# New step orders, three projections in a second PSUM bank, 26 warm-up matmuls, and the int8 result taken out of PSUM by ScalarE: an attention and int8 layer on one core

## What is computed

```python
q, k, v = x @ Wq + bq, x @ Wk + bk, x @ Wv + bv      # 16 query heads, 4 key/value heads, 16 wide
q, k = rope(q), rope(k)                              # per token
p = softmax(causal(q @ k.T * 0.25))                  # 4 query heads share one key/value head
x = layernorm(x + (p @ v) @ Wo)
scale = max(max(abs(x)), 1e-7) / 127.0               # per token
acc = clip(round(x / scale), -128, 127) @ weight.T   # int8 x int8
h = (acc * scale * w_scale + bias).astype(float16)   # w_scale and bias per output column
out = layernorm(x + h)
```

## Time and profile before

| | |
|---|---|
| median of 3 runs | 174.61 us (174.49 to 174.62) |
| the profiled execution's own time | 174.22 us |
| its span, first to last instruction | 172.3 us |
| around the span | 1.9 us |
| mean granted TensorE clock | 0.957 |
| busy in the span | PE 147.3, DVE 140.8, ACT 123.0, POOL 85.7 us |
| in the list: first reduction X0, first exponential E0, end of E159 | 12.59, 19.56, 156.25 us |

### The profile page before, as it was taken

How to read it: one execution, slowest core, us unless ns; L and a number is a source line. 1 busy time by engine, 2 the same in 40 slices (tenths; PEclk the granted TensorE clock), 3 DMA queues, 4 the chain that set the end, 5 groups by cost and what they waited for, 6 DMA issues and landing times. The chain is left out here.

```text
span 172.3 us, 4469 instructions
## 1 busy us (share of the span) xinstructions
PE 147.3 (85%) x1552; PEld 87.3 (51%) x1552; DVE 140.8 (82%) x345; ACT 123.0 (71%) x231; POOL 85.7 (50%) x191
## 2 busy tenths in 40 slices
PE   1768999999999999999999989999999988893330
PEld 0154464565665556656676456655666554551100
DVE  3408789898899599899899789989999997787582
ACT  3244577887797879898988776989878898993000
POOL 1051794224078868213899996032488504465111
PEclk9999999999999999999999999999999999997555
DMA  5986000000000001000000101000001200001101
GB/s 138 259 142 186 2 5 0 4 4 0 10 4 0 6 0 65 1 6 1 2 8 0 56 12 59 8 0 8 0 2 47 80 4 2 2 4 61 61 0 61
DMA packets 5463, 5.63 MB, mean 33 GB/s; under 512 B 1217, under 2 KB 4674, under 8 KB 5442
## 3 DMA queue, kind: packets, MB, share of 16 engines
q1 hardware_dynamic: 5298, 5.16, 10.9%
q10 hardware_dynamic: 144, 0.20, 0.4%
HBM read 3.12 MB, written 2.10 MB: 30 GB/s over the span
## 5 line engine op out<-in xcount | busy, mean ns | idle before, releaser
L415 ACT ACTIVATE prob<-score_ps 128x512 bf16<-128x512 f32 x160 | 89.6, 600 | 16.8 <-PE score_ps L616 8.2
L507 DVE TENSOR_REDUCE nmax<-front_ps 128x1 f32<-128x320 f32 (+21 forms) x137 | 87.6, 680 | 13.2 <-PE front_ps L660 12.3
L612 PE MATMUL score_ps<-qkA 128*128 128x512 bf16 x160 | 57.9, 379 | 0.9 <-ACT prob L415 0.5
L658 PE MATMUL front_ps<-qkA 128*128 128x384 bf16 (+9 forms) x176 | 50.6, 334 | 1.7 <-DVE nmax L507 1.4
L627 PEld LDWEIGHTS mix_ps<-qkv,prob 128*128 128x128 bf16 x640 | 26.1, 96 | 14.3 <-ACT prob L415 3.5
L660 PE MATMUL front_ps<-tab 128*128 128x32 bf16 (+2 forms) x176 | 32.3, 187 | 0.0
L627 PE MATMUL mix_ps<-qkv,prob 128*128 128x17 bf16 x640 | 30.2, 171 | 1.3 <-ACT prob L415 1.2
L658 PEld LDWEIGHTS front_ps<-qkA 128*128 128x128 bf16 x176 | 17.2, 98 | 16.6 <-issue 6.8
L616 PE MATMUL score_ps<-tab 128*128 128x512 bf16 x64 | 24.2, 378 | 0.0
L424 ACT ACTIVATE qkA<-side_ps 128x1024 bf16<-128x1024 bf16 x16 | 16.4, 1024 | 5.5 <-PE side_ps L649 5.3
L354 POOL TENSOR_TENSOR rot<-qkv,tab 128x320 bf16<-128x320 bf16 x14 | 10.4, 745 | 18.6 <-ACT qkv L420 18.6
(11 more groups left out here) (61 smaller groups left out, 175.6 us busy)
## 6 DMA issues: line engine op xcount, KB each, us to landing
out<-fo SPq DMA_DIRECT2D x7, 256.0 KB, 2.2
xt<-in_xT SPq DMA_DIRECT2D x1, 768.0 KB, 6.3
qkA<-peakT SPq DMA_DIRECT2D x32, 4.0 KB
xt<-in_xT SPq DMA_DIRECT2D x2, 128.0 KB, 3.0
bfc<-in_bias SPq DMA_DIRECT2D x2, 128.0 KB, 7.4
out<-fo SPq DMA_DIRECT2D x2, 128.0 KB, 1.7
tab<-in_table SPq DMA_DIRECT2D x1, 232.0 KB, 3.1
wqkv<-in_wqkv_in ACTq DMA_DIRECT2D x1, 192.0 KB
```

Source lines behind the costliest of these rows:

```text
L415: act.activation(prob[:, u % PROB_RING, :].rearrange("p (h t c) -> p t h c", h=GH, c=SUB), score_ps[u % SCORE_RING][:, :].rearrange("p (t ...
L507: dve.tensor_reduce(to, src, AX.X, ALU.max, negate=True).then_inc(max_ok, 1)
L612: mm = pe.matmul(score_ps[u % SCORE_RING][:, :].rearrange("p (t c) -> p t c", c=TOK), qkA[:, n, GH + g, TOK * j:TOK * (j + 1)], qkA[:, n, ...
L658: pe.matmul(bank, qkA[:, n, t, TOK * i:TOK * (i + 1)], qkA[:, n, GH + g:GH + g + fit, 0:wide], start=True, stop=False)
```

## The change

Nothing of the arithmetic's result is meant to change. These parts are edited:

1. Before it waits for the weights, PE issues 26 matmuls of the one-row tile `ones` with itself (128 columns) into `mix_ps`.
2. P1, P2 and P3 go into `dense_ps` instead of `side_ps`.
3. Steps l0 to l5 move from DVE to ACT. There the two tiles are multiplied with the token's scale alone (an fp32 copy of it, `qscf`, written by one more small DVE operation in B0 to B5). POOL's H0 to H5 begin with one more operation on 128x512 fp32, the product with the column's scale. l6, l7 and l8 stay as they were.
4. The five lists are reordered. `rden` has two slots.

The steps n and d of ACT, r of DVE and N of POOL, which the diff also defines, stand in no list, and `NORM_FAST` is 0, so that they do nothing here.

```diff
+LINEAR_ACT = True
+HEAD_TILES = (1, 2, 3, )
+WARM = 26
+NORM_FAST = 0
 ORDER = {
     "tensor": """
-        P0 P1 P2 T0 T1 F0 F1 F2 F3 F4 T2 F5 F6 G0 F7 F8 F9 P3 F10 F11 F12 P4 S0 S1 F13 F14 F15 P5 S2 F16 F17 T3 F18 S3 F19 F20
+        P0 P1 P2 T0 P3 T1 F0 F1 F2 F3 T2 F4 F5 F6 P4 F7 F8 F9 G0 F10 T3 F11 F12 P5 F13 F14 S0 F15 G1 S1 F16 F17 F18 S2 S3 T4
...
-        S135 U6 W132 W133 W134 S136 W135 S137 M6 G15 W136 S138 W137 S139 W138 S140 W139 S141 W140 S142 S143 D5 W141 S144 W142
-        W143 S145 L5 S146 S147 S148 D6 S149 W144 W145 S150 L6 S151 W146 W147 S152 W148 W149 W150 W151 S153 U7 W152 S154 W153
-        S155 W154 S156 M7 S157 W155 S158 W156 S159 W157 W158 W159 U8 M8 D7 L7 D8 L8
+        W131 S135 F175 S136 U6 W132 S137 W133 W134 W135 S138 W136 M6 G15 S139 S140 W137 W138 S141 W139 S142 W140 S143 W141
+        S144 W142 D5 S145 W143 S146 S147 L5 S148 S149 W144 W145 W146 W147 D6 S150 W148 S151 U7 W149 S152 W150 S153 W151 M7
+        S154 W152 S155 W153 S156 W154 S157 W155 S158 W156 S159 W157 L6 W158 W159 D7 U8 M8 L7 D8 L8
     """,
     "scalar": """
-        p0 p1 p2 t0 t1 t2 f0 p3 p4 E0 E1 p5 E2 t3 E3 f1 t4 E4 E5 p6 E6 E7 t5 E8 E9 f2 E10 E11 t6 E12 E13 E14 E15 p7 E16 E17
+        p0 p1 p2 t0 p3 t1 t2 p4 f0 t3 p5 E0 f1 E1 E2 E3 t4 E4 E5 p6 E6 E7 t5 E8 E9 p7 E10 E11 f2 t6 E12 E13 t7 E14 E15 u0 p8
...
-        E146 E147 E148 E149 E150 E151 E152 E153 E154 u7 E155 E156 E157 E158 E159 u8
+        E143 E144 E145 E146 E147 l5 E148 E149 E150 E151 u7 E152 E153 E154 E155 E156 E157 E158 E159 u8
     """,
     "vector": """
...
-        N13 X135 X136 B5 s6 q5 a6 B6 d5 q6 l5 N14 d6 l6 Z5 H6 s7 Z6 a7 B7 N15 Y6 q7 s8 a8 B8 d7 q8 l7 H7 d8 Z7 l8 H8 Y7 Z8 Y8
+        B5 s6 q5 a6 B6 d5 q6 N14 d6 s7 Z5 a7 B7 q7 l6 N15 d7 H6 s8 Z6 a8 B8 Y6 l7 q8 H7 d8 Z7 l8 H8 Y7 Z8 Y8
     """,
     "gpsimd": """
-        R2 w0 K0 R3 K1 R4 R5 K2 R6 R7 K3 K4 K5 m0 R8 Q0 R9 K6 R10 H0 z0 Y0 R11 K7 m1 K8 Q1 K9 m2 R12 Q2 R13 H1 H2 K10 z1 Y1 z2
-        R14 Y2 R15 m3 K11 K12 Q3 K13 m4 Q4 H3 K14 H4 z3 Y3 z4 Y4 m5 K15 Q5 m6 H5 z5 Y5 m7 z6 m8 z7 z8
+        R2 R3 K0 R4 w0 K1 R5 R6 K2 R7 R8 K3 m0 R9 K4 Q0 K5 R10 H0 K6 z0 Y0 R11 m1 K7 Q1 K8 R12 m2 K9 R13 Q2 H1 R14 K10 z1 H2
+        Y1 z2 m3 Y2 K11 R15 K12 Q3 m4 K13 Q4 H3 H4 K14 z3 Y3 z4 Y4 m5 K15 Q5 m6 H5 m7 z5 Y5 m8 z6 z7 z8
     """,
     "sync": """
-        g0 g1 g2 g3 g4 g5 g6 O0 g7 g8 g9 O1 g10 O2 g11 g12 g13 g14 O3 O4 g15 O5 O6 O7 O8
+        g0 g1 g2 g3 g4 g5 g6 O0 g7 g8 g9 g10 O1 O2 g11 g12 g13 g14 O3 O4 g15 O5 O6 O7 O8
     """,
 }
...
+def in_dense(step):
+    return step[0] in "UMDL" or step[0] == "P" and step[1] in HEAD_TILES
+SIDE_USES = [step for step in steps("tensor") if step[0] in "PTG" and not in_dense(step)]
+DENSE_USES = [step for step in steps("tensor") if in_dense(step)]
...
+        def project_bank(u):
+            if u in HEAD_TILES:
+                return dense_ps, dense_full, dense_free, dense_at("P", u)
+            return side_ps, side_full, side_free, side_at("P", u)
...
                 elif kind == "H":
...
+                    if LINEAR_ACT:
+                        pool.tensor_tensor(fo[:, part, :], fo[:, part, :], wsc[:, :].unsqueeze(1).broadcast_to([128, len(ms), HID]),
+                                           ALU.mult).then_inc(fw_ok, len(ms))
+                        pool.wait_ge(fw_ok, done)
...
+                elif kind == "l":
+                    ms, part, done = tiles_of(u)
+                    act.wait_ge(dense_full, dense_at("L", u) + 1)
+                    for m in ms:
+                        one = act.activation(fo[:, m, :], dense_ps[:, (m - ms[0]) * HID:(m - ms[0] + 1) * HID], ACT.Copy,
+                                             scale=qscf[:, m:m + 1])
+                        one.then_inc(dense_free if m == ms[-1] else fo_ok, 1)
...
                     dve.wait_ge(qsc_ok, done)
+                    if LINEAR_ACT and u not in FAST:
+                        dve.tensor_copy(qscf[:, part], qsc[:, part])
...
         @block.tensor
         def _(pe):
             pe.wait_ge(ones_set, 1)
+            for _ in range(WARM):
+                pe.matmul(mix_ps[:, 0:128], ones[:, :], ones[:, :], start=True, stop=True)
             pe.wait_ge(weights_in, 16 * 2)
```

More of the change, by code:

```diff
@@ L86 @@
[L86 to L97, removed]
@@ new lines @@
+        S91 F130 F131 S92 P15 S93 W87 S94 W88 W89 W90 W91 F132 F133 S95 F134 S96 W92 W93 F135 W94 F136 U4 G11 S97 F137 S98
+        F138 W95 W96 M4 S99 W97 S100 G12 F139 S101 F140 S102 F141 S103 F142 S104 F143 T15 S105 S106 F144 W98 W99 W100 W101
+        W102 W103 F145 F146 D3 S107 F147 S108 L3 G13 S109 W104 W105 W106 S110 W107 F148 F149 S111 F150 W108 S112 W109 W110
+        F151 F152 D4 F153 S113 W111 F154 S114 W112 L4 F155 S115 S116 F156 F157 F158 W113 W114 S117 W115 S118 F159 F160 S119
+        W116 S120 F161 W117 W118 S121 F162 S122 W119 F163 S123 G14 F164 S124 F165 U5 S125 W120 W121 W122 S126 W123 F166 M5
@@ L106 @@
[L106 to L109, removed]
@@ L207, in build @@
         prob = sb("prob", [128, PROB_RING, 512], bf16)
-        rden = sb("rden", [128, HEADS], fp32)
+        rden = sb("rden", [128, 2, HEADS], fp32)
         att = sb("att", [128, ALL, HID], bf16)
@@ L226, in build @@
         qsc = sb("qsc", [128, ALL], bf16)
+        qscf = sb("qscf", [128, ALL], fp32)
+        mixs = sb("mixs", [128, 2, HEADS * VA], fp32)
         qrec = sb("qrec", [128, ALL], fp32)
@@ L369, in _ @@
                                        ALU.add).then_inc(roped_ok, 1)
+                elif kind == "N":
+                    pool.wait_ge(den_ok, u + 1)
+                    shares = mixs[:, u % 2, :].rearrange("p (h c) -> p h c", c=VA)
+                    pool.tensor_tensor(att[:, u, :].rearrange("p (h d) -> p h d", d=DH), shares[:, :, 0:DH],
+                                       rden[:, u % 2, :].unsqueeze(2).broadcast_to([128, HEADS, DH]), ALU.mult).then_inc(att_ok, 1)
                 elif kind == "K":
@@ L418, in _ @@
                 elif kind == "p":
-                    act.wait_ge(side_full, side_at("P", u) + 1)
-                    act.activation(qkv[:, u, :, 0:VAT + DH], side_ps[:, 0:PC].rearrange("p (g c) -> p g c", g=GROUPS),
-                                   ACT.Copy).then_inc(side_free, 1)
+                    bank, filled, freed, uses = project_bank(u)
+                    act.wait_ge(filled, uses + 1)
+                    act.activation(qkv[:, u, :, 0:VAT + DH], bank[:, 0:PC].rearrange("p (g c) -> p g c", g=GROUPS),
+                                   ACT.Copy).then_inc(freed, 1)
                 elif kind == "t":
@@ L441, in _ @@
                         one.then_inc(dense_free if m == ms[-1] else x1_ok, 1)
+                elif kind == "n":
+                    act.wait_ge(weighed, LAST_SCORE[u] + 1)
+                    need(act, att_ok, u - 1)
+                    act.activation(mixs[:, u % 2, :], mix_ps[:, 0:HEADS * VA], ACT.Copy).then_inc(mixed_ok, 1)
+                elif kind == "d":
+                    ms, part, done = tiles_of(u)
+                    act.wait_ge(dense_full, dense_at("D", u) + 1)
+                    act.activation(q8T[:, KC * ms[0]:KC * done, :],
+                                   dense_half[:, 0:KC * TOK * len(ms)].rearrange("p (a c) -> p a c", c=TOK),
+                                   ACT.Copy).then_inc(dense_free, 1)
+                elif kind == "l":
+                    ms, part, done = tiles_of(u)
+                    act.wait_ge(dense_full, dense_at("L", u) + 1)
[3 more added lines that the diff above has]
+                        one.then_inc(dense_free if m == ms[-1] else fo_ok, 1)
                 elif kind == "Y":
@@ L512, in _ @@
                                       ALU.subtract).then_inc(peak_ok, 1)
+                elif kind == "r":
+                    dve.wait_ge(mixed_ok, u + 1)
+                    dve.reciprocal(rden[:, u % 2, :], mixs[:, u % 2, :].rearrange("p (h c) -> p h c", c=VA)[:, :, DH])\
+                        .then_inc(den_ok, 1)
                 elif kind == "N":
+                    if u in range(1, NORM_FAST + 1) and NORM_FAST:
+                        dve.wait_ge(att_ok, u)
                     dve.wait_ge(weighed, LAST_SCORE[u] + 1)
-                    dve.reciprocal(rden[:, :], mixed[:, :, DH]).then_inc(den_ok, 1)
+                    dve.reciprocal(rden[:, u % 2, :], mixed[:, :, DH]).then_inc(den_ok, 1)
                     dve.wait_ge(den_ok, u + 1)
                     dve.tensor_tensor(att[:, u, :].rearrange("p (h d) -> p h d", d=DH), mixed[:, :, 0:DH],
-                                      rden[:, :].unsqueeze(2).broadcast_to([128, HEADS, DH]), ALU.mult).then_inc(att_ok, 1)
+                                      rden[:, u % 2, :].unsqueeze(2).broadcast_to([128, HEADS, DH]), ALU.mult).then_inc(att_ok, 1)
                 elif kind == "s":
@@ L623, in _ @@
                     if u == FIRST_SCORE[tile]:
-                        need(pe, att_ok, tile)
+                        if tile <= NORM_FAST:
+                            need(pe, mixed_ok, tile)
```

(9 more changed lines are left out.)

54 lines of the change are left out of this document (33 added, 21 removed).

## The result

The changed kernel took 165.98 us in the median (165.88 to 166.03) against 174.62 for the kernel before on the same chip: a ratio of 0.9506, interval [0.9489, 0.9522], 8.6 us faster. The forecast was 171.5 with a range of 168.6 to 175.0; the direction was right and the size was 2.8 times the forecast's.

What follows compares the result with a forecast made beforehand. No engine was taken as full; the densest, DVE up to 139 us and ACT behind it, set the pace. Middle -3.4 (head's start included), F175 to E159 +0.4, tail -0.1: -3.1, from 174.61 to 171.5 us, range 168.6 to 175.0.

Steps and rivals of the forecast that it cites:

- The head, X0 2.5 us earlier: Start of the kernel: with warm-up and new bank the first reduction X0 comes near 10.1 us instead of 12.59.
- I take it that it does: Head: assumed one-row warm-up matmuls raise TensorE's clock, giving 2.4 GHz from about P1; no run had shown it.
- The third rival: Head: the warm-up doesn't work or the clock falls again; X0 at 11.3, -1.9 in all, 172.7 us; chance 0.10.
- E0 1.8 us earlier: Head: the first exponential near 17.8 us instead of 19.56, a smaller gain because K0 stands behind R3.
- Up to F175, -3.4: Middle, up to the last row maxima: 3.4 us gained, taken between -6.4 (DVE alone) and +2.5 (ACT at 84%).
- ACT is now the dense engine: Middle: ACT taken as dense engine at 88% busy, 117.7 us, 3.4 us earlier with the start.
- POOL's multiplications at nothing: Middle: five multiplications of 1.27 us each, 6.4 us on POOL, counted as hidden because R14 is ahead of H2.
- The fourth rival: POOL stands in DVE's way, holding q or stretching l, H, Z: +2.8 on DVE, 172.4 us; chance 0.06.
- F175 to E159, +0.4: Last maxima to last exponential, ACT the path: l5 adds 1.0, fewer gaps give 0.6 back; sum +0.4.
- The tail, -0.1: Behind E159: N15 earlier gives -1.1, delays of d7, Z6, Y6 and l7 take it back; bounds -1 and +1.6.
- Rival 1: Whole kernel: DVE alone set the pace; -6.4 in the middle, -6.1 in all, 168.5 us; chance 0.18.
- Rival 2: Up to F175: ACT becomes the bound, slower; +2.5, with l5 in full +1.0, 178.1 us; chance 0.14.

Runs made afterwards that it cites:

- run d: The changed kernel with l0 to l5 back on DVE, without small copies or extra POOL multiplication, lists otherwise as changed: 168.65 us, ratio 0.9674.
- i: The changed kernel with two more 128x256 copies on ACT behind each of l0 to l4: 167.22 us, ratio 0.9600.
- j: The changed kernel with two more 128x256 statistics operations on DVE at each of five places: 167.28 us, ratio 0.9592.
- run a: The kernel before, old lists, no head bank or warm-up; only l0 to l5 moved to ACT, with POOL's extra multiplication: 183.04 us, ratio 1.0468.
- run k: The changed kernel with one step of POOL's list moved, m7 behind z5 and Y5 as in the old list: 169.63 us, ratio 0.9732.
- c: The changed kernel without the 26 warm-up matmuls: 165.76 us, ratio 0.9495.
- l: The changed kernel with the 26 warm-up matmuls on 128 rows of ones instead of one row: 164.59 us, ratio 0.9463.

## Why the prediction was wrong, step by step

- **The head, X0 2.5 us earlier: 0.9.** The step that failed is "I take it that it does", that one-row matmuls raise the clock. They did not. With full rows the other numbers of that step are nearly met or passed: X0 at 9.2, where 10.1 was reckoned. The third rival, that the warm-up does nothing, gave X0 at 11.3; it was 11.67 in this profile, 11.30 to 11.32 in five others with the same head, and 11.21 without the warm-up. That rival had the head right. The bank's mechanism (P1 right behind P0, R3 behind R2) was right.
- **E0 1.8 us earlier: 0.1.** E0 waits for the peaks through G0 and f0 and stands behind F14 on PE; it follows the clock and the maxima. Yet the new bank was worth more than E0 shows: without it the time is 3.8 us longer, part of which can be a later rise of the clock. I had taken the first exponential as the price of the head.
- **Up to F175, -3.4: -6.4.** This carried the miss, and two steps failed. The first is "ACT is now the dense engine": I held ACT's and DVE's shares against each other and disposed of PE with "PE's work is the same, its start 2.4 earlier". The runs show PE nearest to the pace: 3.5 us for 4.3 of work there, 1.2 and 1.3 for some 3 on ACT and DVE. ACT reached 89%, which I had allowed, without being the bound. The second is that the new order "S ahead of its W" and the other moves "are in the -3.4", a sum made of loads alone, so that they stood at nothing. With l still on DVE (run d) the stretch from X0 to X136 is already 3.2 us shorter; the move of l adds 2.2.
- **Why the move of l pays is open.** From d to the changed kernel DVE's busy time falls by 3.9 us (139.4 to 135.5) and ACT's rises by 3.8 (121.7 to 125.5). At the nearly equal prices of i and j that comes to about nothing, and the time fell by 2.7. So it is not the load; the waits of d say that l on DVE makes PE and ACT wait longer, but no run moved l's place alone.
- **The size of l on ACT.** Reckoned at 0.51 us each; 12 took 5.0, 0.42 each:

```profile
L485 ACT ACTIVATE fo<-dense_ps,qscf 128x256 f32<-128x256 f32 x12 | 5.0, 467 | 0.0
...
L418 POOL TENSOR_TENSOR fo<-fo,wsc 128x512 f32<-128x512 f32 x6 | 7.6, 1270 | 7.8 <-ACT fo L485 7.8
```

- **POOL's multiplications at nothing: right here** (0.4 us at most), at the 1.27 us each that had been read, and with the cover that was named: R14 ahead of H2. What it costs when the cover is gone was priced at "up to 1.3 each"; the old lists show 6.1 to 6.5 for all six, with one place in a where a late rope stops PE and the clock falls behind it, at 4.0 us. The fourth rival, POOL holding up DVE's own operations, is not seen: DVE's q took 0.32 us in the mean, not longer than before.
- **F175 to E159, +0.4: -0.8** (from the end of X136). l5 stands in ACT's chain as said. But the 2.06 us of idle time in the window fell to 0.99, 1.1 less where 0.6 was taken, and the window holds 28 operations of ACT with l5's two, against 29 before: some three exponentials now lie ahead of it, which the sum did not have.
- **The tail, -0.1: -1.1.** The step about m7 was right as a condition, as run k shows (3.7 us if it is broken). The delays that I charged (d7, Z6, Y6 and l7 ahead of q8: +1.0) were too dear: with N15's second operation 0.8 us earlier, Y8 ends 1.1 earlier.
- **The rivals.** Rival 1 gave -6.4 for the middle, and that is what came, but by luck: 3 us more on DVE cost only 1.3 to 1.5, so DVE does not set the pace. Rival 2, ACT as the bound and 178.1, has no support. With l on ACT in the old lists the kernel does get slower (183.0 us), but mostly through POOL's list, not through ACT's load.

## What to carry to other kernels

When several engines hand work to each other through one in-order list, don't choose the pace-setter by comparing busy shares. Follow the chain that ended last, compare the gaps between the starts of PE's matmuls, and if it can be run, add a few microseconds to each engine and see what comes through; read from the profile how much was really added. A step moved to another engine is worth as much as the lists make of it: the same move gained 2.7 us or lost 8.4, and most of the loss came by way of a third engine's list. A warm-up should be made of matmuls like those that follow, and its effect read from the duration of the first real ones.

## What the runs showed that was not expected

Twenty-six matmuls of one row and 128 columns, back to back from 1.03 us, left TensorE at 1.2 GHz until 12.31 us (11.1 to 13.6 in the six other profiles with them, 11.38 in c without); the same with 128 rows had it at 2.4 GHz by 4.14. In run a a stop of 2.0 us in the middle of the kernel (104.8 to 106.7) was followed by 3.4 us at the lower level; the longest stop in the middle before it had been 1.1 us. The Trainium skill, page "TensorE: Matmul & The Clock Gate", section "Part 1: The HAM clock gate", says that activity releases the throttle and idleness brings it back. Both are seen here, at 4.14 us in l and at 106.7 in a. That one-row matmuls did not release it is what these runs add.
